# Row factors of the SwiGLU parts on GpSimd, their normalization on ScalarE, and the first part joined to the load stage

## The reference

```
def _layernorm(x, axis=-1, eps=1e-05):
    m = jnp.mean(x, axis=axis, keepdims=True)
    v = jnp.var(x, axis=axis, keepdims=True)
    return (x - m) / jnp.sqrt(v + eps)
...
        gate = jnp.einsum('bsd,hd->bsh', x, wg)
        up = jnp.einsum('bsd,hd->bsh', x, wu)
        h = jax.nn.silu(gate) * up
        return jnp.einsum('bsh,dh->bsd', h, wd)
...
    x = L0_attn_x
    x = x + 0.5 * _L0_ffn_ref(_layernorm(x, axis=-1), L0_ffn_w_gate, L0_ffn_w_up, L0_ffn_w_down)
    x = x + _L0_attn_ref(_layernorm(x, axis=-1), ...)
    x = x + 0.5 * _L0_ffn_ref(_layernorm(x, axis=-1), L0_ffn_w_gate, L0_ffn_w_up, L0_ffn_w_down)
    x = x + 0.5 * _L1_ffn_ref(_layernorm(x, axis=-1), L1_ffn_weights, L1_ffn_scale, L1_ffn_bias)
    x = x + _L1_attn_ref(_layernorm(x, axis=-1), ...)
    x = x + 0.5 * _L1_ffn_ref(_layernorm(x, axis=-1), L1_ffn_weights, L1_ffn_scale, L1_ffn_bias)
```

## Time and profile before

| | us |
|---|---|
| Median of 3 runs | 1502.01 (1501.01 to 1511.87) |
| The profiled execution | 1511.9 |
| Its span in the trace | 1510.1 |
| TensorE busy | 1179.1 (78%) |
| VectorE busy | 1015.7 (67%) |
| GpSimd busy | 612.7 (41%) |
| ScalarE busy | 540.8 (36%) |

### The profile page before, as it was taken

One profiled execution on the slowest core, in us unless ns is written; L12 is line 12 of the kernel. 1 busy time (PEld: TensorE's weight loads), 2 busy tenths in 40 slices (PEclk: granted clock), 3 DMA queues, 4 the chain that ended last, 5 costly groups with the idle time before them and its releaser, 6 DMA issues. The chain is left out here.

```text
span 1510.1 us, 42845 instructions
## 1 busy us (share of the span) xinstructions
PE 1179.1 (78%) x17314; PEld 850.4 (56%) x17314; DVE 1015.7 (67%) x2796; ACT 540.8 (36%) x1367; POOL 612.7 (41%) x1286
## 2 busy tenths in 40 slices
PE   0788887675688888888888888675888879589968
PEld 0667776532455555565565555454676766335546
DVE  5556656327767877788888867763556654589963
ACT  0221212322445555555555545353222216131033
POOL 1223330064345655656666655333332323240035
PEclk9989995576888999989899888888889998799979
DMA  7000001001222222212222222210000002566002
GB/s 191 0 1 1 1 0 47 7 8 29 57 58 59 53 57 55 49 31 54 57 59 59 59 58 52 57 33 2 1 0 1 1 9 62 149 155 176 23 15 98
DMA packets 192741, 71.23 MB, mean 47 GB/s; under 512 B 139296, under 2 KB 187808, under 8 KB 192544
## 3 DMA queue, kind: packets, MB, share of 16 engines
q1 hardware_dynamic: 190944, 65.87, 18.8%
q10 hardware_dynamic: 1600, 2.62, 0.6%
HBM read 43.03 MB, written 21.23 MB: 43 GB/s over the span
## 5 line engine op out<-in xcount | busy, mean ns | idle before, releaser
L470 POOL TENSOR_TENSOR ffn_H<-ffn_hid,ffn_H 128x512 fp32r<-128x512 f32 x96 | 124.8, 1300 | 270.9 <-DVE ffn_H L445 270.9
L1523 DVE TENSOR_TENSOR delta_tmp<-delta_PR 128x30 f32<-128x30 f32 (+14 forms) x480 | 174.8, 364 | 10.3 <-DVE ln_mean_var L295 0.3
L1525 DVE TENSOR_TENSOR delta_PR<-delta_PR,delta_tmp 128x30 f32<-128x30 f32 (+14 forms) x480 | 171.8, 358 | 11.5
L411 ACT ACTIVATE ffn_silu<-psum 128x512 f32<-128x512 f32 x96 | 57.5, 599 | 206.5 <-PE psum L374 206.5
L441 DVE TENSOR_TENSOR ffn_hid<-ffn_silu,psum 128x512 f32<-128x512 f32 x96 | 66.0, 688 | 88.9 <-PE psum L374 86.8
L374 PE MATMUL psum<-ffn_XT,w_gate 128*128 128x512 f32 x384 | 118.5, 434 | 3.9 <-DVE ffn_XT L433 3.9
L1391 ACT ACTIVATE delta_wide<-delta_S 32x128 f32<-32x128 f32 x256 | 78.5, 307 | 104.5 <-DVE delta_S L1545 51.2
L374 PE MATMUL psum<-ffn_XT,w_up 128*128 128x512 f32 x384 | 114.0, 422 | 0.0
L339 PE MATMUL psum<-consts,ffn_xn 128*128 128x128 f32 x128 | 26.2, 371 | 94.7 <-DVE ffn_xn L311 94.7
L387 PE MATMUL psum<-w_down,ffn_H 128*128 128x256 f32 x768 | 95.8, 285 | 5.3 <-POOL ffn_H L470 5.3
L387 PEld LDWEIGHTS psum<-w_down,ffn_H 128*128 128x128 f32 x768 | 95.1, 191 | 7.4 <-POOL ffn_H L470 6.2
(11 more groups left out here) (273 smaller groups left out, 2690.4 us busy)
## 6 DMA issues: line engine op xcount, KB each, us to landing
within_scratch<-delta_PT SPq DMA_DIRECT2D x128, 64.0 KB, 2.0
delta_PR<-within_scratch SPq DMA_DIRECT2D x16, 512.0 KB, 4.4
inverse_scratch<-delta_PR SPq DMA_DIRECT2D x16, 512.0 KB, 5.3
delta_T<-inverse_scratch SPq DMA_DIRECT2D x128, 64.0 KB, 2.4
space_T<-taps_scratch SPq DMA_DIRECT2D x8, 1024.0 KB, 6.2
X<-taps_scratch SPq DMA_DIRECT2D x8, 1024.0 KB, 9.0
X<-in_x SPq DMA_DIRECT2D x32, 128.0 KB, 10.2
late_X<-X SPq DMA_DIRECT2D x64, 64.0 KB, 2.0
```

The lines of the kernel that those rows point to most:

```text
L411: a.activation(M.silu[n % 3], B.bank[n % 2][:], ACT.Silu, scale=1.0 / 127.0).then_inc(S.silu, 1)
L470: g.tensor_tensor(lo.bitcast(F32R), M.hid[n % 3], hi, ALU.subtract).then_inc(S.hid_lo, 1)
L1523: i = v.tensor_tensor(t3, column.to_broadcast([P, j, n_after]), row.to_broadcast([P, j, n_after]), ALU.mult)
L1525: i = v.tensor_tensor(after, after, t3, ALU.add)
```

## The change

The stages start and ffn 0 become one stage, `first`, with no barrier between them. Its buffers are those of ffn and the raw weights together. In it VectorE computes the statistics of only the first three blocks ahead (AHEAD = 3); those of block b+3 stand behind m = 2 to 5 of block b, one tile each. GpSimd computes the row factors of a block after its statistics (`first_factors`), for blocks 0 to 2 in between the three weight casts. TensorE waits for each weight's cast (`w_ready`).

In both SwiGLU passes `prep` is split. `rows(b)`, the normalization, is ScalarE's (Identity, scale, bias), and stands behind `gate_up(b-1, 1)`; `turn(b)`, the rest of `prep`, stands where `prep` stood. GpSimd computes the factors of the new `X` for the next stage, block by block (`new_factors(b-1)` behind its low part of m = 4 of block b, the last one at the end). ffn 1 and space begin with one call of the four instructions for all 32 tiles on GpSimd; gates and binary 0 compute no factors any more. VectorE no longer waits for its own mean-variance instruction in `tile_stats`.

```
-        plan = (("start", 0), ("ffn", 0), ("gates", 0), ("delta", 0), ("ffn", 1), ("binary", 0), ("space", 0), ("binary", 1))
+        plan = (("first", 0), ("gates", 0), ("delta", 0), ("ffn", 1), ("binary", 0), ("space", 0), ("binary", 1))
...
+def first_vector(v, own, B, M, S, run):
     v.wait_ge(S.consts_in, 16)
+    for b in range(AHEAD):
+        for j in range(BLK):
+            first_stats(v, own, B, S, b, j)
...
+def first_gpsimd(g, own, B, M, S, run):
+    own.seq(g.memset(B.minus_half[:], -0.5))
+    first_factors(g, own, B, S, 0)
+    for i, w in enumerate((B.w_gate, B.w_up, B.w_down)):
+        g.wait_ge(S.raw_in[i], 16)
+        g.tensor_copy(w[:].bitcast(F32R), M.raw[i].bitcast(I32)).then_inc(S.w_ready, 1)
+        if i < AHEAD - 1:
+            first_factors(g, own, B, S, i + 1)
+    ffn_gpsimd(g, own, B, M, S, run)
...
+def row_factors(g, own, B, MV, t0, t1):
+
+    rstd, shift = B.rstd[:, t0:t1], B.shift[:, t0:t1]
+    g.tensor_scalar(shift, MV[:, t0:t1, 0], -1.0, None, ALU.mult)
+    own.seq(g.tensor_scalar(rstd, MV[:, t0:t1, 1], 1e-5, None, ALU.add))
+    own.seq(g.tensor_tensor(rstd, rstd, B.minus_half[:, t0:t1], ALU.pow))
+    return g.tensor_tensor(shift, shift, rstd, ALU.mult)
...
 def tile_stats(v, own, B, X, MV, t):
     s = B.stats[:, 6 * (t % BLK):6 * (t % BLK) + 6]
     own.seq(v.bn_stats(s, X[:, t, :]))
-    own.seq(v.bn_aggr(MV[:, t, :], s))
...
+    return v.bn_aggr(MV[:, t, :], s)
...
-def ffn_order(gate_up, prep, down):
-
-    prep(0)
+def ffn_order(gate_up, rows, turn, down):
+
+    rows(0)
+    turn(0)
     for b in range(NBLK):
         for m in range(MH):
             gate_up(b, m)
-            if m == 1 and b > 0:
-                down(b - 1)
+            if m == 1:
+                if b > 0:
+                    down(b - 1)
+                if b + 1 < NBLK:
+                    rows(b + 1)
             if m == 3 and b + 1 < NBLK:
-                prep(b + 1)
+                turn(b + 1)
     down(NBLK - 1)
...
 def ffn_scalar(a, own, B, M, S, run):
...
+    def rows(b):
+        a.wait_ge(S.f_rstd, b + 1 if run == 0 else NBLK + 1)
+        if blocks + b > 0:
+            a.wait_ge(S.xt_ps, 2 * (blocks + b))
+        for j in range(BLK):
+            t = BLK * b + j
+            i = a.activation(M.xn[:, j * DM:(j + 1) * DM], B.X[:, t, :], ACT.Identity, bias=B.shift[:, t:t + 1], scale=B.rstd[:, t:t + 1])
+        i.then_inc(S.xn, 1)
...
 def ffn_gpsimd(g, own, B, M, S, run):
...
+    if run == 1:
+        row_factors(g, own, B, B.MV, 0, NT).then_inc(S.f_rstd, 1)
...
         g.tensor_tensor(lo.bitcast(F32R), M.hid[n % 3], hi, ALU.subtract).then_inc(S.hid_lo, 1)
...
+        if m == MH - 2 and b > 0:
+            new_factors(b - 1)
+        if run == 0 and m == MH - 1 and b + AHEAD < NBLK:
+            first_factors(g, own, B, S, b + AHEAD)
...
 def space_gpsimd(g, own, B, M, S, run):
     beta_row = B.rows[3]
+    row_factors(g, own, B, B.MV2, 0, NT).then_inc(S.n_rstd, 1)
```

More of the change, by code:

```diff
@@ L192, in tensor @@
         def tensor(eng):
-            steps = {"start": start_tensor, "ffn": ffn_tensor, "gates": gates_tensor, "delta": delta_tensor, "binary": binary_tensor,
+            steps = {"first": first_tensor, "ffn": ffn_tensor, "gates": gates_tensor, "delta": delta_tensor, "binary": binary_tensor,
                      "space": space_tensor}
@@ L200, in scalar @@
             own = Own(eng, S.act)
-            steps = {"start": start_scalar, "ffn": ffn_scalar, "gates": gates_scalar, "delta": delta_scalar, "binary": binary_scalar,
+            steps = {"first": first_scalar, "ffn": ffn_scalar, "gates": gates_scalar, "delta": delta_scalar, "binary": binary_scalar,
                      "space": space_scalar}
@@ L208, in vector @@
             own = Own(eng, S.dve)
-            steps = {"start": start_vector, "ffn": ffn_vector, "gates": gates_vector, "delta": delta_vector, "binary": binary_vector,
+            steps = {"first": first_vector, "ffn": ffn_vector, "gates": gates_vector, "delta": delta_vector, "binary": binary_vector,
                      "space": space_vector}
@@ L216, in gpsimd @@
             own = Own(eng, S.pool)
-            steps = {"start": start_gpsimd, "ffn": ffn_gpsimd, "gates": gates_gpsimd, "delta": delta_gpsimd, "binary": binary_gpsimd,
+            steps = {"first": first_gpsimd, "ffn": ffn_gpsimd, "gates": gates_gpsimd, "delta": delta_gpsimd, "binary": binary_gpsimd,
                      "space": space_gpsimd}
@@ L223, in sync @@
         def sync(eng):
-            steps = {"start": start_sync, "gates": gates_sync, "delta": delta_sync, "binary": binary_sync, "space": space_sync}
+            steps = {"first": start_sync, "gates": gates_sync, "delta": delta_sync, "binary": binary_sync, "space": space_sync}
             for n, (kind, run) in enumerate(plan):
@@ L379, in down @@
         pe.wait_ge(S.hid_lo, base + MH * b + MH)
+        if run == 0 and b == 0:
+            pe.wait_ge(S.w_ready, 3)
         for j in range(BLK):
@@ L411, in gate_up @@
         a.activation(M.silu[n % 3], B.bank[n % 2][:], ACT.Silu, scale=1.0 / 127.0).then_inc(S.silu, 1)
-    def down(b):
-        pass
-    ffn_order(gate_up, prep, down)
+    ffn_order(gate_up, rows, turn, nothing)
 def ffn_vector(v, own, B, M, S, run):
@@ L453, in down @@
             v.wait_ge(S.x_new, tiles + t + 1)
-            tile_stats(v, own, B, B.X, B.MV, t)
-    ffn_order(gate_up, prep, down)
+            i = tile_stats(v, own, B, B.X, B.MV, t)
+        i.then_inc(S.f_done, 1)
+    ffn_order(gate_up, nothing, turn, down)
 def ffn_gpsimd(g, own, B, M, S, run):
@@ L461, in ffn_gpsimd, with new_factors @@
     base = MH * blocks
-    def prep(b):
-        pass
+    if run == 1:
+        row_factors(g, own, B, B.MV, 0, NT).then_inc(S.f_rstd, 1)
+    def new_factors(b):
+        g.wait_ge(S.f_done, blocks + b + 1)
+        row_factors(g, own, B, B.MV, BLK * b, BLK * b + BLK)
     def gate_up(b, m):
@@ L929, in gates_vector @@
     bank, seq = B.bank, own.seq
-    norm_factors(v, own, B, B.MV)
     for b in range(NBLK):
```

110 lines of the change are left out of this document (47 added, 63 removed).

## The result

The changed kernel takes **1434.53 us** (median of four runs, 1428.34 to 1437.74); the kernel before takes 1506.94 (median of four, 1501.01 to 1515.31; three of the four are the executions told of above). The ratio is 0.951, with a 95% interval of 0.945 to 0.958. Forecast were 1436, in 1412 to 1459, and faster.

What follows compares the result with a forecast made beforehand. TensorE was taken to bound the kernel, waiting in SwiGLU passes for VectorE's late normalization. Terms -49.8 - 23.1 - 2.9 + 4.9 = -70.9 gave 1441 from 1511.9, or 1431; the middle, 1436, was forecast, range 1412 to 1459.

Steps and rivals of the forecast that it cites:

- What bounds: SwiGLU passes: TensorE waits 94.7 us before transposes for VectorE's late normalization; a block could cost 18.0 instead of 21.5 to 24.0.
- The head: Start of the first pass: fewer statistics and no Newton ahead, so the first product comes at 23.0 instead of 44.17.
- The blocks: Both SwiGLU passes: 18.4 to 18.9 us between transposes at clock 1.00; first pass -49.8, ffn 1 -23.1.
- The waits of `down`: TensorE waits for GpSimd's low part of m = 5: 0.5 a block, 0.8 in the first pass, 4.0 at the last.
- The root by its width: Head of ffn 1 and space: GpSimd's root is paid by column, so 32 columns take 6.9 us.
- Rival B: The root costs by instruction, not column: both 32-tile calls take 1.9 instead of 7.8, total 1424; chance 0.20.
- gates: Head of gates: Newton's 2.7 us go, but the first transposes wait for the weights' DMA; gain 0.
- binary 0: Start of binary 0: ScalarE starts at once instead of 3.0 after the stage's begin; -2.9.
- space: Start of space: 3.0 us before ScalarE starts become 7.8 + 0.1 with the 32-tile factors; +4.9.
- The sum: Whole kernel: -70.9, giving 1441 from the profiled 1511.9, or 1431 by the median; 1436 is the middle.
- VectorE and GpSimd: Shared port lock: casts to `H` may wait out GpSimd instructions; price nothing, 17 if every 1.04 root met the path.
- Rival D: GpSimd's factor sets mid-pass cost far more, making the kernel slower; 14 to 21 per extra us on a set; chance 0.03.

Runs made afterwards that it cites:

- vector_ahead: The changed kernel with the four normalizations kept on VectorE, at the early place where ScalarE has them; 1435.51 us.
- scalar_late: The changed kernel with ScalarE's four normalizations moved back behind `gate_up(b, 3)`, where VectorE's stood before; 1459.46 us.
- all_stats_first: The changed kernel with statistics and factors of all eight blocks ahead of the first pass instead of three (AHEAD = 8); 1444.51 us.
- before_again: The kernel before, unchanged, profiled a second time; 1500.52 us.
- gates_padded: The changed kernel with twelve small value-preserving VectorE instructions at the head of gates, where Newton stood; 1435.58 us in one execution.
- factors_behind_2: The changed kernel with `new_factors(b-1)` behind GpSimd's low part of m = 2 instead of m = 4; 1420.08 us.
- factors_twice: The changed kernel with every `new_factors` set in the passes computed twice in a row; 1486.86 us in one execution.

## Why the forecast held, step by step

**What bounds.** That the passes were set by the normalization's late place is shown twice: moved ahead on either engine it makes nothing wait between the heads (the changed kernel and vector_ahead), moved back on ScalarE it returns as a wait of 1.7 (scalar_late). The forecast put ScalarE's part at "hidden behind Silu of m = 1, beside `down`"; it is.

**The head.** Forecast 23.0, measured 22.61, by way of two errors that partly cancel. ScalarE was to load a table behind its wait, 1.28; it loaded it at 2.92, long before, `xn` started at 15.96, 0.04 behind the factors, and the transposes at 18.18 instead of 19.1. Then VectorE, still at its statistics and casts until 21.27, held the subtraction for `XT` by more than the 0.5 counted: 22.61 less 18.18 is 4.4, where 3.35 + 0.5 stood in the sum. Most of that surplus is one cast: `ident_r`, counted at 0.2, took 0.61, beside GpSimd's cast of `w_up`, and ended 0.08 behind it (timeline of the head, above). In all_stats_first, beside a root, it takes 0.20 (rows below, under VectorE and GpSimd). Another size was misread and hardly shows: the dropped waits in `tile_stats` were put at some hundredths each and are 0.15 a tile (block 0 takes 2.22, from 11.60 to 13.82, where it took 2.67, from 11.19 to 13.86); the later landing of its rows took most of that back.

**The blocks.** Forecast 18.4 to 18.9 at a clock of 1.00, measured 18.70. The waits of `down`: 0.5 in ffn 1 and 0.8 in the first pass were forecast, and 0.72 came in both (one of 0.90), so the statistics in the first pass do not push VectorE back in a way that reaches `down`. The last wait, 4.0, came as 4.05 and 4.28, and the `down` behind it takes 7.47 and 7.42 in both passes, where 0.8 less was taken for the second. From the first product to the end of the first pass 159.4 passed, 158.4 were forecast. The first pass gave -49.2 of -49.8, against a base that another execution puts 5.8 lower (before_again): the close match is in part luck.

**The root by its width.** The split was mis-sized. The forecast took 0.20 fixed and 0.21 for each column, 6.9 on 32. Four widths are measured now: 1.04 on 4, 1.67 on 8, 3.56 on 20 and 5.46 on 32. From 4 to 32 columns that is 4.42 over 28, 0.158 a column, and 0.41 is left as fixed; 8 columns then give 1.67 and 20 give 3.57. The product on the same shape (0.20) was a bad measure of the root's fixed part. Rival B, one price for any width, is out. What GPSIMD Engine Reference of the Trainium skill (section 3.1) gives for 28 more columns of a two-input operation, 0.06 us as an estimate, fits the multiplication behind the root (0.20 on 4 columns, 0.25 on 32) and not the root: there the measurement is 4.42. The first product of ffn 1 so came 1.1 earlier than forecast (12.2 against 13.3), but what follows it took 158.1 instead of 156.1: 1.3 more in the six waits (4.3 against 3.0) and 0.8 in the last `down`. -22.2 stands against -23.1.

**gates, binary 0, space.** gates 0: shown by gates_padded. binary 0: -3.0 at its start, and -3.7 for the stage, against -2.9. space: ScalarE starts 6.7 after the stage's begin instead of 3.0, so +3.7, and from that begin to the end of the kernel it is 4.4 longer, against +4.9. Over the profiles of all the changed kernels with this code binary 0 takes 61.1 to 63.4 and the rest 204.5 to 209.4, so these two single differences are known to some 2 us.

**The sum against its base.** The sum was -70.9. The medians differ by 72.4, the two profiles by 83.5. The forecast left open whether the 9.9 by which its profile lay above the median would be taken off; they lay mostly in delta (before_again is 10.9 shorter there), so taking them off was right, and the halfway value of 1436 was 5 above what the sum gives from the median of then, 1502.0. That the measured median still is near 1436 owes something to the kernel before having a median of 1506.94 in this comparison, by one more execution of 1515.31: 1506.9 less 70.9 is 1436.0. Seven executions beside the later runs have medians of 1502.8 and 1504.8, from which the change would take 68 to 70. So the match of the 1436 itself is luck by some us. The sum was right within some 3 us, in a measurement that knows the difference to some 10 (the ratio's interval), and its base to no better than 5.

**VectorE and GpSimd.** The lock that the prediction describes, by which one of the two engines waits for the other, was forecast at a price of nothing. The casts to `H` of the changed kernel in the first pass, duration in ns, minimum, median, maximum, and from its timeline the longest with the GpSimd row beside it:

```profile
L478 DVE CAST first_H<-first_hid x48: 426/427/1457, 27.2 to 168.5; 128x512 fp32r<-128x512 f32 x48
```
```profile
42.34 1.30 POOL L515 TENSOR_TENSOR first_H<-first_hid,first_H 128x512 fp32r<-128x512 f32 x1
...
42.46 1.46 DVE L478 CAST first_H<-first_hid 128x512 fp32r<-128x512 f32 x1
```

The median is 0.427, the longest 1.457. It starts 0.12 behind a GpSimd instruction of 1.30 and ends 0.28 behind it, as if it had waited for its end. The rule of the Trainium skill (SBUF — State Buffer, "Who interferes with whom") says just that, and these rows agree with it. So do all 122 casts to `H` of the ten profiles that begin with more than 0.3 us left of a GpSimd subtraction: none takes less than 0.58. The root does not hold a cast in this way, as two rows of all_stats_first show:

```profile
31.19 1.04 POOL L322 TENSOR_TENSOR ln_rstd<-ln_rstd,minus_half 128x4 f32<-128x4 f32 x1
...
31.64 0.20 DVE L280 CAST ident_r<-consts 128x128 fp32r<-128x128 f32 x1
```

This cast begins with 0.59 of the root left and takes its usual 0.20. The 21 casts to `H` that begin with more than 0.3 us of a root left all take 0.43. There the rule, by which the first of the two holds the ports for its whole instruction, is not borne out. The prediction took the root as the longest lock that the change adds, 1.04 each and 17 if all met the path; that term was taken from the wrong instruction. The long casts stand beside subtractions, of which the sets push some back: 9 casts begin so in the changed kernel, and 1 in each profile of the kernel before.

In the blocks the lock costs nothing: in ffn 1 six blocks have one cast of 1.37 to 1.39 each, and they take 18.7 with a wait of 0.72, like those of the first pass, where most have none. At the head it does reach the path: 0.4 of the first product's start is the long cast `ident_r`. In factors_behind_2 the cast of 1.00 beside a POOL row of 2.50 reaches it too (1.35 in ffn 1), once a pass. So the price of nothing was right for the blocks of the changed kernel, and 0.4 too low at its head.

**Rival D's price.** Each us more on a set was put at 7 a pass, and up to 7 more in the first for its second set, 14 to 21 in all, so that D would decide at 3 to 5 us more. factors_twice shows 25.5 and 25.9 a pass for 2.1 us. The second set is not on the path (at 60.19 it runs beside `down`), but the clock is, and it was left out, as was the last set's own 2.1 at the end of the pass. D would have decided at about 66 / 25, 2.6 us more. Its condition did not come: the set shown above takes 2.3 (56.62 to 58.88) where it took 1.92 in binary 1.

## What to carry to other kernels

When an engine waits in every block for a small chain, first look at where the chain stands in its engine's in-order list, before asking which engine should do it: the same operations on ScalarE cost 0 or 24 us here by two places in a list, and at the early place VectorE did nearly as well; only at the late place did the engine matter. The same goes for what fills an idle engine: a 2 us set of small operations cost 13 us in front of the one item that `down` waits for, and it stood nearly free two items earlier, where 0.9 us of the last wait in each pass are left of it. And before counting a gain at a stage's head, look for the transfer that ends last there.
